# Softmax numerators scaled before they are split, instead of the attention output after

## The reference

```python
x = x + tanh(g_xattn) * xattn(layernorm(x), ctx, mask)
x = x + tanh(g_ffn)   * ffn(layernorm(x))
# xattn
q, k, v = x @ W_q, context @ W_k, context @ W_v          # split in 8 heads of 64
sim  = where(mask, q k^T * 64**-0.5, -max)
attn = softmax(sim)                                      # over 750 keys
out  = (attn v) @ W_o + b_o
# ffn, twice "bitlinear": rmsnorm, rows rounded to 8 bits, weights rounded to -1, 0, 1
h = gelu(bitlinear(x, w1, b1)); y = bitlinear(h, w2, b2) # 512 -> 2048 -> 512
```

## Time and profile before

| | |
|---|---|
| median of 3 runs | 1072.07 us (1071.88 to 1073.18) |
| the profiled execution | 1070.9 us; span of its instructions 1069.1 us |
| busy, share of the span | PE 93%, DVE 78%, ACT 75%, GpSimd 67% |
| PE busy from 100 to 1000 us | 868.08 of 900 us |
| granted TensorE clock | 0.99 of full |

### The profile page before, as it was taken

How to read it: one execution, slowest core, us unless ns; L and a number is a source line. 1 busy time by engine, 2 the same in 40 slices (tenths; PEclk the granted TensorE clock), 3 DMA queues, 4 the chain that set the end, 5 groups by cost and what they waited for, 6 DMA issues and landing times. The chain is left out here.

```text
span 1069.1 us, 26540 instructions
## 1 busy us (share of the span) xinstructions
PE 995.9 (93%) x9856; PEld 579.5 (54%) x9856; DVE 835.2 (78%) x1707; ACT 805.7 (75%) x1374; POOL 712.1 (67%) x691
## 2 busy tenths in 40 slices
PE   3988899999999999999999998999999999999877
PEld 2455565565555655555556555556565565555443
DVE  4788798778798777777779876788878776886976
ACT  3976787977878668796868867697786977777766
POOL 5577998577676776567576575767668666956651
PEclk9999999999999999999999999999999999999989
DMA  7989999787879979697877986988867889868750
GB/s 225 280 163 228 206 170 174 133 184 128 163 142 180 174 116 192 115 167 162 157 129 126 200 163 130 183 143 139 177 128 158 175 162 171 167 110 139 148 96 30
DMA packets 472335, 169.17 MB, mean 158 GB/s; under 512 B 450320, under 2 KB 452368, under 8 KB 471824
## 3 DMA queue, kind: packets, MB, share of 16 engines
q1 hardware_dynamic: 472208, 167.48, 80.5%
HBM read 48.28 MB, written 7.34 MB: 52 GB/s over the span
## 5 line engine op out<-in xcount | busy, mean ns | idle before, releaser
L1339 POOL TENSOR_TENSOR p<-prob,p 128x750 f16<-128x750 f32 x224 | 358.5, 1614 | 110.4 <-ACT p L1189 108.1
L1007 DVE CUSTOM_DVE_ANT_0 prob<-ps_s,mbias 128x750 f32<-128x750 f32 x224 | 204.0, 933 | 58.8 <-PE ps_s L820 47.1
L1182 ACT ACTIVATE prob<-prob,rmin 128x750 f32<-128x750 f32 x224 | 204.3, 914 | 26.2 <-DVE rmin L1007 25.8
L787 PE MATMUL ps_g<-ctx,wk 128*128 128x375 f16 x1152 | 201.8, 327 | 23.4 <-POOL ctx L1350 16.4
L787 PE MATMUL ps_g<-wv,ctx 128*128 128x512 f16 (+1 forms) x864 | 197.0, 379 | 4.1 <-DVE k_sb L1026 2.2
L787 PEld LDWEIGHTS ps_g<-ctx,wk 128*128 128x128 f16 x1152 | 111.2, 99 | 105.6 <-issue 25.7
L820 PE MATMUL ps_s<-k_sb,q_sb 64*32 64x375 f16 (+2 forms) x2688 | 128.8, 322 | 15.6 <-DVE rmin L1007 15.4
L787 PEld LDWEIGHTS ps_g<-wv,ctx 128*128 128x128 f16 (+1 forms) x864 | 86.8, 103 | 101.0 <-issue 5.9
L849 PE MATMUL ps_g<-pt,v_sb 128*64 128x224 f16 (+2 forms) x2448 | 122.8, 254 | 2.6 <-DMA pt<-p 2.4
L1189 ACT ACTIVATE p<-prob 128x750 f16<-128x750 f32 x144 | 116.0, 820 | 3.5 <-DMA pt<-p 3.0
L849 PEld LDWEIGHTS ps_g<-pt,v_sb 128*64 128x64 f16 x2448 | 109.6, 110 | 2.9 <-issue 2.8
(11 more groups left out here) (134 smaller groups left out, 1524.6 us busy)
## 6 DMA issues: line engine op xcount, KB each, us to landing
ctx_f<-in_ctx SPq DMA_DIRECT2D x47, 375.0 KB, 4.0
xa<-in_x SPq DMA_DIRECT2D x16, 448.0 KB, 4.7
xr<-in_x SPq DMA_DIRECT2D x28, 256.0 KB, 3.4
out<-xr SPq DMA_DIRECT2D x28, 256.0 KB, 2.8
pt<-p SPq DMA_TRANSPOSE x254, 4.0
h_sb<-in_w SPq DMA_DIRECT2D x4, 512.0 KB, 4.6
w<-in_w SPq DMA_DIRECT2D x3, 512.0 KB, 5.0
xr<-in_w SPq DMA_DIRECT2D x3, 512.0 KB, 5.4
```

The costliest lines, as they stand in the source:

```text
L787: mm = nc.tensor.matmul(out, lhs, rhs, start=(m == 0), stop=(m == len(steps) - 1))
L1007: nc.vector.tensor_tensor_reduce(prob[:, (b * NU + n) % PROBS, :].rearrange("p (c k) -> p c k", c=2), ps_s[:, n % 2, :, 0:CH], mbias[:, :] ...
L1182: nc.scalar.activation(prob[:, (b * NU + n) % PROBS, :], prob[:, (b * NU + n) % PROBS, :], ACT.Exp, bias=rmin[:, n:n + 1], scale=-1.0, acc ...
L1339: nc.gpsimd.tensor_tensor(p16[:, u % HILO, 1, 0:J], prob[:, (b * NU + n) % PROBS, :], p16[:, u % HILO, 0, 0:J], ALU.subtract).then_inc(s[" ...
```

## The change

The row sums' reciprocals are used before the split. After E of both units of a score step, VectorE takes the two reciprocals (128x2) and scales each by 512 in place (128x1, twice). H is on ScalarE for all 14 units and multiplies by the reciprocal while it makes the upper half (`scale=rrec[:, n:n + 1]`). GpSimd's L has two instructions: a 128x750 float32 multiplication of `prob` by the reciprocal in place, and the subtraction as before. The weighted sum is then final up to the factor 1/512: ScalarE and VectorE split it straight from PSUM (PL: upper half on ScalarE, PA: lower half on VectorE), and the 640 small matmuls, the buffers `rrec16` and `att`, the copy on ScalarE, VectorE's multiplication and GpSimd's PL are gone. `prob` stays at 5 units and `p16` at 4. All five tables are new.

```diff
-    "O": ("x2", 1), "V": ("v_lo", 1), "F1": ("h_lin", NF), "PV": ("attn_raw", 1), "Q": ("q_lo", 1),
+    "O": ("x2", 1), "V": ("v_lo", 1), "F1": ("h_lin", NF), "PV": ("attn_lo", 2), "Q": ("q_lo", 1),
...
-HI_ON_ACT = [n for n in range(NU) if n not in (2, 5, 7, 10, 12)]
...
                 elif kind == "PV":
 
-                    need(pe, "recips", b, recips_for(b, n))
-                    j, first_query, size, row = weighs(b, n)
-                    for m in units_of(b, n):
-                        for of, q, at, many in pieces_of(b, m):
-                            if of != j or not first_query <= q < first_query + size:
-                                continue
-                            to = 256 + q - first_query
-                            for a in range(2):
-                                for e in range(2):
-                                    u = 2 * m + e
-                                    nc.tensor.matmul(g[e * DH:(e + 1) * DH, to:to + many],
-                                                     rrec16[:, a, u:u + 1].to_broadcast([128, DH]),
-                                                     ident[:, at:at + many], start=(a == 0), stop=(a == 1))
+                    j, _, size, row = weighs(b, n)
                     for m in units_of(b, n):
                         for e in range(2):
                             need_turned(pe, b * NU + 2 * m + e)
...
+            def take_reciprocals(b, m):
+
+                need(dve, "expd", b, 2 * m + 1)
+                need(dve, "p_lo", b - 1, 2 * m + 1)
+                nc.vector.reciprocal(rrec[:, 2 * m:2 * m + 2], rsum[:, 2 * m:2 * m + 2]).then_inc(s["recips_raw"], 1)
+                need(dve, "recips_raw", b, m)
+                for u in (2 * m, 2 * m + 1):
+                    nc.vector.tensor_scalar(rrec[:, u:u + 1], rrec[:, u:u + 1], RS, None, ALU.mult)\
+                        .then_inc(s["recips"], 1)
...
                 elif kind == "PA":
-                    need(dve, "recips_out", b, n)
-                    qs = slice(0, queries_of(b, n))
-                    nc.vector.tensor_tensor(att[:, qs], g[:, qs], att[:, qs], ALU.mult)\
-                        .then_inc(s["attn_raw"], 1)
+                    pieces = attn_pieces(b, n)
+                    need(dve, "attn_hi", b, 2 * n + 1)
+                    for at, to, size in pieces:
+                        nc.vector.scalar_tensor_tensor(out=attn[:, 1, n % NP, to:to + size], in0=g[:, at:at + size],
+                                                       scalar=1.0 / RS, in1=attn[:, 0, n % NP, to:to + size],
+                                                       op0=ALU.mult, op1=ALU.subtract)\
+                            .then_inc(s["attn_lo"], 2 // len(pieces))
...
+                elif kind == "H":
 
                     u = b * NU + n
-                    need(act, "expd", b, n)
+                    need(act, "recips", b, n)
                     need_turned(act, u - HILO)
-                    nc.scalar.activation(p16[:, u % HILO, 0, 0:J], prob[:, (b * NU + n) % PROBS, :], ACT.Copy)\
-                        .then_inc(hi_act, 1)
-                elif kind == "PV":
+                    nc.scalar.activation(p16[:, u % HILO, 0, 0:J], prob[:, (b * NU + n) % PROBS, :], ACT.Copy,
+                                         scale=rrec[:, n:n + 1]).then_inc(s["p_hi"], 1)
+                elif kind == "PL":
...
+                        nc.scalar.activation(attn[:, 0, n % NP, to:to + size], g[:, at:at + size], ACT.Copy,
+                                             scale=1.0 / RS).then_inc(s["attn_hi"], 2 // len(pieces))
...
+                    held = prob[:, u % PROBS, :]
+                    need(pool, "p_hi", b, n)
+                    nc.gpsimd.tensor_scalar(held, held, rrec[:, n:n + 1], None, ALU.mult).then_inc(s["normed"], 1)
+                    need(pool, "normed", b, n)
+                    nc.gpsimd.tensor_tensor(p16[:, u % HILO, 1, 0:J], held, p16[:, u % HILO, 0, 0:J], ALU.subtract)\
+                        .then_inc(s["p_lo"], 1)
```

Of the tables, the line of GpSimd's list in which L:0:7 stands, before and after:

```diff
-    L:10:6 PL:0:6 H:12:6 L:11:6 L:12:6 G2:1:5 PL:1:6 XB:0:6 L:13:6 L:0:7 L3:1:5 H:2:7 XB:1:6 PL:2:6 L:1:7 L:2:7
+    L2:1:5 L:8:6 G2:0:5 L:9:6 L:10:6 MB:0:7 L3:0:5 L3:1:5 N1:0:8 L:11:6 L:12:6 L:13:6 XB:1:6 L:0:7 G2:1:5 CX:0:8
```

More of the change, by code:

```diff
@@ L147 @@
[L147 to L151 removed]
+    K:0:0 K:1:0 K:2:0 K:3:0 Q:0:0 Q:1:0 S:0:0 Q:2:0 K:4:0 S:1:0 V:0:0 K:5:0 K:6:0 V:1:0 S:2:0 V:2:0 V:3:0 V:4:0
@@ L460, in emptied @@
         return name, tile_of(b, n // times) * times + n % times + 1
-    return name, b * PER_BATCH[name] + n + 1
-HI_ON_ACT = [n for n in range(NU) if n not in (2, 5, 7, 10, 12)]
-HI_ON_POOL = [n for n in range(NU) if n not in HI_ON_ACT]
+    return name, b * PER_BATCH[name] + times * (n + 1)
 def build(nc, x_d, ctx_d, mask_d, gx_d, gf_d, wq_d, wk_d, wv_d, wo_d, bo_d, w1_d, b1_d, w2_d, b2_d, out_d):
@@ L527, in build @@
         rrec = sb("rrec", [128, NU], F32)
-        rrec16 = sb("rrec16", [128, 2, NU], F16)
         p16 = sb("p16", [128, HILO, 2, JP], F16)
         pt = sb("pt", [128, 2, 2 * NT, RING_ROWS], F16)
-        att = sb("att", [128, TQ], F32)
         attn = sb("attn", [128, 2, NP, RINGQ], F16)
@@ L1177, in emit @@
                 p = b % 2
-                g = bank(kind, n, b) if kind in EMPTIED else None
+                filled = {"PL": "PV"}.get(kind, kind)
+                g = bank(filled, n, b) if filled in EMPTIED else None
                 if kind == "E":
@@ L1200, in emit @@
                     for at, to, size in pieces:
-                        nc.scalar.activation(attn[:, 0, n % NP, to:to + size], att[:, at:at + size], ACT.Copy)\
-                            .then_inc(s["attn_hi"], 2 // len(pieces))
+                        nc.scalar.activation(attn[:, 0, n % NP, to:to + size], g[:, at:at + size], ACT.Copy,
+                                             scale=1.0 / RS).then_inc(s["attn_hi"], 2 // len(pieces))
                 elif kind == "K":
@@ L1328, in emit @@
                 p = b % 2
-                if kind == "H" and n in HI_ON_POOL:
+                if kind == "L":
                     u = b * NU + n
-                    need(pool, "expd", b, n)
-                    need_turned(pool, u - HILO)
-                    nc.gpsimd.tensor_copy(p16[:, u % HILO, 0, 0:J], prob[:, (b * NU + n) % PROBS, :]).then_inc(hi_pool, 1)
-                elif kind == "L":
-                    u = b * NU + n
-                    need_hi(pool, b, n)
-                    nc.gpsimd.tensor_tensor(p16[:, u % HILO, 1, 0:J], prob[:, (b * NU + n) % PROBS, :],
-                                            p16[:, u % HILO, 0, 0:J], ALU.subtract).then_inc(s["p_lo"], 1)
-                elif kind == "PL":
-                    pieces = attn_pieces(b, n)
-                    for m, (at, to, size) in enumerate(pieces):
-                        need(pool, "attn_hi", b, 2 * n + (1 if m == len(pieces) - 1 else 0))
-                        nc.gpsimd.tensor_tensor(attn[:, 1, n % NP, to:to + size], att[:, at:at + size],
-                                                attn[:, 0, n % NP, to:to + size], ALU.subtract)\
-                            .then_inc(s["attn_lo"], 2 // len(pieces))
+                    held = prob[:, u % PROBS, :]
[4 more added lines that the diff above has]
+                        .then_inc(s["p_lo"], 1)
                 elif kind == "CX":
```

505 lines of the change are left out of this document (234 added, 271 removed).

## The result

| | kernel before | changed kernel |
|---|---|---|
| median of the runs | 1071.97 us (1071.46 to 1073.18) | 1220.96 us (1217.69 to 1222.25) |
| ratio | | 1.138, 95% interval 1.136 to 1.141 |
| profiled execution's span | 1069.1 us | 1218.3 us |

The account below looks back on a forecast made before the run. TensorE, 96.5% busy from 100 to 1000 us, was taken as the bound: 1070.9 - 15.4 (matmuls) + 0.5 (ends) = 1056.0 us profiled, and 1.2 more gives the median, 1057.2; range 1045 to 1080, 8 in 10.

Parts of the forecast that it names:

- GpSimd's multiplication: On GpSimd, 224 new 128x750 float32 multiplications at 0.829 us each, +185.7 us of busy time; upper end +259.
- rival E: Chain through five prob buffers becomes the pace, M waiting for GpSimd, score steps for M: +28 us, 1085; chance 0.24.
- VectorE "not on the path: 0": VectorE's cheaper reciprocals and more PA pieces: net -12 us of its work, worth 0 in the time.
- GpSimd's hold on VectorE's work on x: Shared SBUF interfaces stretch VectorE's splits and centrings of x: at worst 5 us, beside TensorE's work.
- TensorE: -15.4: Removing 640 small matmuls in 68 groups from TensorE saves 15.4 us, all counted; far end 26.6.
- Rival D: TensorE's list doesn't set the pace, so fewer matmuls only make idle time: 1072 us; chance 0.06.
- ScalarE, +66, not on the path: ScalarE's upper halves with operand, minus copies to att: net +66 us to about 872, 82.5% busy, no bound.
- Rival C: ScalarE at 82.5% empties PSUM banks later, eating some 15 us of the saving: 1072 us; chance 0.05.
- The longer chain of a unit: 0: Softmax chain from E through reciprocals and multiplication grows 1.5 to 2.3 us per pair, covered by other work: 0.
- The signs: Right: TensorE still 96% busy from 100 to 1000 us, multiplication 0.81 to 0.85 us; wrong: 1.1 or more, or under 94%.

Follow-up runs that it names:

- experiments 2 and 4: 2: changed kernel, GpSimd's multiplication given a second operation, times 1.0: 1037.87 us. 4: kernel before plus one-operation GpSimd multiplication ahead of each subtraction: 1360.29 us.
- experiment 5: Kernel before with its tables, without the 640 small matmuls, ScalarE copying the weighted sum instead of the spread reciprocals: 1070.07 us, ratio 0.997.
- Experiment 8: Kernel before without the two scalings of the reciprocals to float16 on VectorE, small matmuls reading a buffer of ones: 1044.39 us, ratio 0.973.
- two-operation kernel: Changed kernel with one line edited, a second operation (times 1.0) in GpSimd's multiplication: 1037.87 us, ratio 0.968.
- experiment 3: Changed kernel without GpSimd's multiplication, lower halves made from unscaled numerators: 1019.55 us, ratio 0.950.

## Why the prediction was wrong, step by step

**GpSimd's multiplication: the step that failed.** The prediction took 0.829 us from the cast of the same width and 1.158 as the upper end from L1323. It measured 2.207. The term was +185.7 us and is +494.3. The sentence that chose it, "same width and one input", picked the wrong likeness: L1323, the only `TENSOR_SCALAR` at such a width in the rows, has two operations, and so it bounded a two-operation multiplication (0.929 measured, inside the range) but not one with a single operation. No other row could have helped: all five `tensor_scalar` lines of GpSimd in the kernel before (L1323, L1357, L1363, L1379, L1393) have two operations. A row bounds another form only if nothing that may matter differs. The price alone makes the loss (experiments 2 and 4), through the place that rival E named: M waits for a `prob` buffer, S waits for M. E's price, one step in four losing 1 us, was too small: 164 us over 112 score steps is 1.5 us at every step. GpSimd became the pace itself: it is busy 843.9 of the 900 us in the middle, and it makes up 75% of the chain that ended last. So the rival's mechanism was right and its size was not: it put 28 us on the forecast, and the measured time is 164 above it (1221.0 - 1057.2). The Trainium skill (GPSIMD Engine Reference, Engine selection) calls one-input elementwise work on GpSimd roughly line-rate. That fits the two-operation form and the copy (895 and 808 ns for 750 columns), not the one-operation form.

**VectorE "not on the path: 0": the second step that failed.** It hid behind the first. The prediction saw that the old scalings were dear and irregular, and took 84.75 to 65.3 us; they became 41.7. (The forecast took 0.214 us for a 128x1 scaling, from L1090; the new ones take 0.149.) But it gave the difference no worth, because VectorE was 78% busy. Taking 71.5 us off VectorE in the old kernel gave 29.1 us; putting 48.9 on in the new one (802.6 to 851.5) cost 18.9; putting 29.1 on (831.7) cost 9.6. That is 0.33 to 0.41 us of time per us of VectorE's work, three times over. So changes of this size on an engine that is 78% busy, and that stands between PSUM and TensorE at every step, cost or gave a third of their length or more. The 5 us put down for GpSimd's hold on VectorE's work on x were low as well: with the two-operation multiplication the two centrings take 56.5 us where they took 44.7, and the split 40.6 where it took 42.0.

**TensorE: -15.4.** The price of the matmuls was right (14.3 us at full clock, experiment 5); "so I count all of it" was not. They were worth 2.8 us in the old list and 9.2 in the new, and in the old list the rest went into idle time and into a lower clock. (The last batch has six groups of four and two of eight, not four and four; that hardly moves the sum.) The view behind it, "in the long middle almost nothing but TensorE's own work sets the time", rested on the busy share of 96.5%. Experiment 8 refutes it: the same list with the same matmuls runs 2.7% faster when only VectorE has less to do. Nor is a busy time the work alone: the same 9216 matmuls are 1022.5 us busy in the changed kernel and 979.5 in the two-operation one. 36 of these 43 us are clock: TensorE is busy for 87.7 us at 1.2 GHz in the one and for 15.7 in the other. The trace agrees here with what the Trainium skill (Perfetto Trace Analysis, Identifying the Most-Contended Engine) says of the busy share, which the prediction cited and then set aside. The reasons that these runs show are waits and the clock. Rival D, at 0.06, held for most of the 15 us in the old list and for 6 of them in the new one.

**ScalarE, +66, not on the path.** 865.9 us measured, 872 forecast; the upper half with the operand takes 913 - 820 = 93 ns more, forecast 94. Rival C did not come: in the two-operation kernel ScalarE is at 83% and the kernel is faster.

**The longer chain of a unit: 0.** With the cheap multiplication it isn't 0 but at best covered in part: taking the multiplication out altogether gives 18.3 us more (experiment 3), which holds both its length in the chain and its load on GpSimd. These two were not told apart.

**The signs.** "Wrong: a multiplication at 1.1 us or more, or a middle in which TensorE falls under 94%" was what came: 2.2 us, and 87%. What the prediction had described was in truth experiment 2, with a multiplication at 0.93: forecast 1057.2, measured 1037.9. On that kernel the terms compare as follows. VectorE has 32.6 us less work than before (835.2 to 802.6), at 0.39 worth -13 us where 0 was put. The matmuls gave 6 us less than counted. The multiplication cost 18 where 0 was put. The short way out of PV and what the removals do only together (-6.1 and -8.6 with the old tables) were not counted. That balance is about -3 us, and the measured difference -19. The last two are the least certain of the terms, and those from the old tables need not hold in the new ones. The 16 us between stay open; the new tables are the part that no run here measured by itself, since no kernel was run with the new division and the old tables.

## What to carry to other kernels

Price an instruction from a row of the very form, down to the number of operations in it; where no such row exists the upper end is open, and a run of that form alone is worth more than any reasoning on its neighbours. Small VectorE instructions beside a busy GpSimd should be read by their longest time, not their mean: where the spread is tenfold and the ends coincide with GpSimd's, they can be made cheap (one input, one column here), and the gain was on the path here even at 78% busy. And TensorE's busy share does not prove that TensorE sets the pace: count the matmuls that pass in a fixed stretch when another engine's load changes, and take the granted clock beside every busy time.

## What the runs showed of the hardware

- GpSimd's `TENSOR_SCALAR` with one operation takes 2171 ns for 128x750 float32 and with two operations 895 (alone, nothing beside it); at 1024 columns 2847 and 1117. A multiplication by 1.0 as second operation took 15% off the time of the whole kernel (1220.96 to 1037.87 us).
- GpSimd's `TENSOR_TENSOR` with a column broadcast as second input took 1435 ns for the same work, also less than the one-operation form.
- VectorE's 128x1 `TENSOR_SCALAR` was never held by GpSimd (145 to 149 ns in 64), its 128x4 form was (158 to 1451), and `SCALAR_TENSOR_TENSOR` on SBUF was at 128x1 too (161 to 1617).
- With less work the granted clock came out lower: without its 640 small matmuls the old kernel had TensorE busy for 33.6 us at 1.2 GHz where it was 19.3, and that hid 7 of their 14 us.
